# Cross attention of a Perceiver block: 2048 scores at a time in one group of four PSUM banks, and another order of its first slots

## What is computed

```python
# x 256x512 (normalised), cond 4096x512, 16 heads of 32
q = (x @ Wq + bq) * 32**-0.5;  k, v = split(cond @ Wkv + bkv)
q = quantise(q, per row);  k = quantise(k, per row)     # round(x / s) * s, s = absmax / 127
v = quantise(v, per column over the tokens)
a = softmax(q @ k.T)                                     # per head 256 x 4096
a = round(a / (max(a) / 255)) * (max(a) / 255)
out = (a @ v) @ Wp + bp
```

## Time and profile before

| what | us |
|---|---|
| median of 3 runs (lowest, highest) | 582.43 (581.07, 583.52) |
| span of the profiled execution | 582.8 |
| busy in it: PE, DVE, ACT, POOL | 531.9, 457.6, 364.7, 28.4 |
| first scores of the cross attention to its last exponentials' start | 128.95 to 361.46 |

### The profile page before, as it was taken

The page is one execution under the profiler, slowest core; times in us unless marked ns, Lnnn a source line. Parts: engine busy times, 40 slices in busy tenths (PEclk is TensorE's granted clock), DMA queues, the critical chain, the costliest instruction groups (busy, mean ns, idle before and its releaser), DMA issues. The chain is left out here.

```text
span 582.8 us, 10649 instructions
## 1 busy us (share of the span) xinstructions
PE 531.9 (91%) x4283; PEld 333.8 (57%) x4286; DVE 457.6 (79%) x858; ACT 364.7 (63%) x431; POOL 28.4 (5%) x28
## 2 busy tenths in 40 slices
PE   3999999999899999999998788699999899996995
PEld 2444555543566656665665565488884565652582
DVE  2599999966899989998999797401593889878995
ACT  5624656464799889988998788400343753586342
POOL 0300000000300200030005100000000000000000
PEclk9999999999999999999998788899999999997999
DMA  8723300042345435553556459603938204300000
GB/s 319 264 74 87 130 1 1 0 142 85 119 148 182 165 107 176 166 168 112 160 177 241 170 165 432 265 1 95 319 163 341 106 0 180 111 0 0 2 2 36
DMA packets 20145, 78.84 MB, mean 135 GB/s; under 512 B 2176, under 2 KB 3200, under 8 KB 16896
## 3 DMA queue, kind: packets, MB, share of 16 engines
q1 hardware_dynamic: 20096, 78.16, 37.8%
HBM read 75.27 MB, written 0.79 MB: 131 GB/s over the span
## 5 line engine op out<-in xcount | busy, mean ns | idle before, releaser
L1122 DVE CUSTOM_DVE_ANT_0 arena<-ps,arena 128x1024 f32<-128x1024 f32 x128 | 152.5, 1220 | 16.2 <-issue 7.7
L1530 ACT ACTIVATE arena<-arena,small 128x4096 int16<-128x4096 f32 x32 | 121.5, 3798 | 2.5 <-DVE small L1135 2.4
L600 PE MATMUL ps<-arena 128*128 128x512 f16 x384 | 100.1, 380 | 0.0
L641 PE MATMUL ps<-small,arena 128*128 128x128 bf16 x1024 | 81.7, 225 | 8.1 <-DVE arena L1142 4.8
L566 PE MATMUL ps<-arena 128*128 128x512 f16 x384 | 85.2, 379 | 1.2 <-DVE arena L1053 1.2
L641 PEld LDWEIGHTS ps<-small,arena 128*128 128x128 bf16 x1024 | 61.1, 100 | 17.8 <-issue 6.9
L1537 ACT ACTIVATE arena<-ps 128x512 int32<-128x512 int32 x96 | 56.9, 593 | 21.7 <-PE ps L641 21.3
L815 PE MATMUL ps<-arena 128*128 128x256 f32 (+1 forms) x288 | 67.3, 397 | 0.7 <-ACT arena L1619 0.7
L815 PEld LDWEIGHTS ps<-arena 128*128 128x128 f32 x288 | 55.7, 194 | 11.8 <-issue 3.3
L566 PEld LDWEIGHTS ps<-arena 128*128 128x128 f16 x384 | 37.2, 98 | 43.6 <-issue 1.5
L657 PEld LDWEIGHTS ps<-arena 128*128 128x128 f16 x1024 | 43.0, 97 | 30.1 <-issue 8.2
(11 more groups left out here) (172 smaller groups left out, 729.5 us busy)
## 6 DMA issues: line engine op xcount, KB each, us to landing
arena<-key_scales SPq DMA_DIRECT2D x64, 512.0 KB, 5.0
arena<-in_ctxT SPq DMA_DIRECT2D x8, 1024.0 KB, 6.8
arena<-in_wg SPq DMA_DIRECT2D x4, 1024.0 KB, 7.2
arena<-in_wo SPq DMA_DIRECT2D x2, 2048.0 KB, 11.6
arena<-in_wu SPq DMA_DIRECT2D x4, 1024.0 KB, 6.9
arena<-in_wd SPq DMA_DIRECT2D x4, 1024.0 KB, 5.8
arena<-in_wuq SPq DMA_DIRECT2D x1, 3072.0 KB, 24.9
arena<-in_wkr SPq DMA_DIRECT2D x1, 2048.0 KB, 13.9
```

The costliest lines, as they stand in the source:

```text
L600: last = pe.matmul(ps[:, bank, :], wv16[wpart][:, k, g * P:(g + 1) * P], ctx16[cpart][:, k, tok], start=(k == 0 and i == 0), stop=(k == KC ...
L641: last = pe.transpose(ps[:, bank, :].bitcast(BF16)[:, b * P:(b + 1) * P], p16[u % 2][:, (8 * q + b) * P:(8 * q + b + 1) * P].bitcast(BF16) ...
L1122: dve.tensor_tensor_reduce(sc[:, u % 2, i * SCW:(i + 1) * SCW], ps[:, 2 * (n % 2):2 * (n % 2) + 2, :].rearrange("p a b -> p (a b)"), skb[: ...
L1530: act.activation(p16[u % 2], sc[:, u % 2, :], ACT.Exp, bias=ebias[:, u % 2:u % 2 + 1], scale=sq[:, i:i + 1], accum_out=rsum[:, u:u + 1]).t ...
```

## The change

A unit's scores are made in two calls of 2048 keys: four matmuls on the four groups of 32 array rows into banks 0 to 3. There is only this one group of four banks, so call n waits for scaling n-1. DVE scales 2048 at once; the second operation starts its maximum from the result of the first, so `score_max` goes. The ring is 3 loads of 1024 KB. A call of the second half writes the whole region of the int16 exponentials, so it waits for all four transposes of unit u-2. The first three slots are written out by hand (`first_slots`): group 1's first part is projected there, parts 1 to 5 in slots 3 to 7, and parts 6 and 7 both in slot 8. DVE instead of ACT reads three projections of group 0 out, and for groups 1 to 3 stores three of the four v quarters (before two). `turn_values(g, 0)` comes earlier in its slot, `turn_p` and `values` are otherwise in their places.

```diff
-RING = 5
+SPAN = 2 * SCW
+HALVES = 2
+RING = 3
...
-        ORDER = (2, 3, 0, 1)
+        ORDER = (1, 0)
...
+            if s <= 1:
+                return [(0, j, FREE_BANKS[j]) for j in (2 * s, 2 * s + 1)]
+            if s <= SLOTS:
+                return [(1, j, 7) for j in ((6, 7) if s == SLOTS else (s - 2,))]
...
-                if n >= 2:
-                    pe.wait_ge(scu, n - 1)
+                    pe.wait_ge(scu, n)
-                for a in range(2):
-                    row = slice(HD * (2 * cp + a), HD * (2 * cp + a + 1))
-                    last = pe.matmul(ps[:, 2 * (n % 2) + a, :], qT4[row, h, t * P:(t + 1) * P],
+                for a in range(4):
+                    row = slice(HD * a, HD * (a + 1))
+                    last = pe.matmul(ps[:, a, :], qT4[row, h, t * P:(t + 1) * P],
...
                 dve.tensor_tensor_reduce(
-                    sc[:, u % 2, i * SCW:(i + 1) * SCW],
-                    ps[:, 2 * (n % 2):2 * (n % 2) + 2, :].rearrange("p a b -> p (a b)"),
-                    skb[:, load % RING, :], 1.0, -3.0e38, ALU.mult, ALU.max,
+                    sc[:, u % 2, i * SPAN:(i + 1) * SPAN],
+                    ps[:, 0:4, :].rearrange("p a b -> p (a b)"),
+                    skb[:, load % RING, :], 1.0, smax[:, u % 2, 0:1] if k else -3.0e38, ALU.mult, ALU.max,
                     smax[:, u % 2, k:k + 1]).then_inc(scu, 1)
-
-            def score_max(u):
-                dve.wait_ge(scu, (u + 1) * NCH)
-                dve.tensor_reduce(mfin[:, u % 2:u % 2 + 1], smax[:, u % 2, :], AX, ALU.max).then_inc(mf, 1)
...
+                if len(steps) == 2:
+                    store_projected_values(*steps[0])
+                if half == 0:
+                    store_values(group, 0)
```

More of the change, by code:

```diff
@@ L398, in turns @@
[L398 to L403, removed]
+            p = [("p", s - 2, 2), ("p", s - 2, 3), ("p", s - 1, 0), ("p", s - 1, 1)]
+            if s == 2:
+                out = p[:2] + [("v", 0, c) for c in range(NCH)] + p[2:]
+            elif half == 0:
+                out = p[:2] + [("v", g, 0), p[2], ("v", g, 1), p[3]]
+            elif half == 1:
+                out = [p[0], ("v", g, 2), p[1], ("v", g, 3)] + p[2:]
+            else:
+                out = p
@@ L730, in _, with project_part @@
+            first_slots()
+            for s in range(3, UNITS + 2):
                 now = s < UNITS
[L731 to L733 removed]
+                late = s - 2 < UNITS
+                prev = s - 1 < UNITS
+                pieces = [(g, j, bank, k) for g, j, bank in value_steps(s) for k in range(KC)]
+                each = len(pieces) // 4
                 group, half = values_turned_in(s)
[L735 removed]
+                def project_part(n):
+                    for g, j, bank, k in pieces[n * each:(n + 1) * each]:
+                        project_values(g, j, bank, [k])
@@ L736, in _ @@
                 if now:
                     scores(s, 0)
-                    scores(s, 1)
-                for g, j, bank in steps[:1] if s == 0 else []:
-                    project_values(g, j, bank, range(KC))
-                if late:
-                    turn_p(s - 2, 2)
-                for g, j, bank in inline:
-                    project_values(g, j, bank, [0])
-                if late:
-                    values(s - 2, 0)
+                turn_p(s - 2, 2)
+                project_part(0)
@@ L756, in _ @@
                     project_first((s - FIRST_OUT - 3) // 2, [2])
-                for g, j, bank in steps[1:2] if s == 0 else []:
-                    project_values(g, j, bank, range(KC))
-                for g, j, bank in inline:
-                    project_values(g, j, bank, [1])
-                if late:
-                    values(s - 2, 1)
-                if half == 1:
-                    turn_values(group, 3)
-                if now:
-                    scores(s, 3)
+                values(s - 2, 1)
+                if half is not None:
+                    turn_values(group, 3 if half else 0)
                 if s in (FIRST_OUT, FIRST_OUT + 1):
@@ L1218, in _ @@
                     add_first(0)
-                if now:
-                    scale_scores(s, 1)
-                if s == 1:
-                    for g, j, _ in last[2:]:
-                        max_values(g, j)
-                    scale_values(group)
                 if late:
```

260 lines of the change are left out of this document (152 added, 108 removed).

## The result

The changed kernel takes 588.41 us (median of 4 runs, 587.43 to 588.85) beside 582.97 for the kernel before (4 runs, 581.07 to 584.10): ratio 1.0095, 95% interval 1.0071 to 1.0119. It is slower by 5.4 us. The forecast was 588.9 us, with a chance of 0.69 for slower. The 66 runs of the kernel before that were made beside the experiments lie between 580.85 and 586.67 us, so two single runs can differ by 1%, not only by the 0.3% named at the start.

What follows compares the result with a forecast made beforehand. PE, DVE and ACT are nearly full, with a PE-ACT loop setting plain slots. Terms -1.2 + 3.1 - 2.2 + 3.3 + 0.5 + 3.0 = +6.5 gave 589.3 us span, 588.9 median; range 585 to 593, wider 580.5 to 597.

Steps and rivals of the forecast that it cites:

- Plain slots: Sixteen plain steps with a projection: beat 6.46 to 6.38 us, held by a PE-ACT loop of waits; -1.2 us.
- The first rival: Plain slots: the PE-ACT loop does not bind, beat is PE's 6.13 us; 577.9 us in all, chance 0.13.
- The scaling: DVE's scaling of 2048 keys at once: 2.2 us, between 2.0 and 2.44.
- Slot 8: Group 1's parts 6 and 7 both here: twelve more matmuls and a wait for the shared bank; +3.1 us.
- First slots: Opening slots shed 2.6 us of matmuls and 1.3 of scores but gain waits; -2.2 us, bounds 0 and -3.9.
- unit 3 near 164: Sign that the forecast is right: unit 3's exponentials start near 164 us in the profile.
- Boundaries: First two slots of each value group: PE waits for the late value scale, then for DVE's copy and store; +3.3 us.
- The clock: PE's stops of 2.5 and 1.9 us bring one clock fall each in groups 1 and 2; +3.0 us, bounds 0 and 9.
- The third rival: Clock falls often, also in the opening slots and last six units: four more falls, +6, 595 us; chance 0.17.
- The tail and the stage ahead: Slots from unit 26 on, apart from load delays, and the stretch before the first projection of v: no change.
- Loads: Ring loads of 1024 KB land 5.8 us after issue, late only after head 12; +0.5 us, bounds 0 and 1.3.
- the fourth rival: Ring of three starves: 1024 KB broadcasts land in 7.5 us, delaying scalings; +7 on the forecast, 596 us; chance 0.05.

Runs made afterwards that it cites:

- The wide scores alone: Kernel before with only the 2048-key scores in four banks, single scaling and ring of three added; projections and turned values unmoved: 582.39 us, ratio 0.9996.
- the placement alone: Changed kernel with the earlier kernel's 1024-key scores and ring of five, keeping the moved projections, first slots and turned values: 591.78 us, ratio 1.0147.
- the fourth run: Changed kernel with last maximum and value scale made ahead of the first scores' scaling on DVE in a value group's first slot: 586.54 us, ratio 1.0055.
- the third run: Changed kernel with each value projection's last quarter ahead of the first turned probabilities on PE, its ACT read-out ahead of their first copy: 589.54 us, ratio 1.0105.
- two edits: Changed kernel with earlier last projection quarter and read-out, plus value scale ahead of the first scaling in a group's first slot: together 583.44 us, ratio 1.0013.

## Why the prediction was right, point by point

**Plain slots: right, and shown.** 6.46 became 6.40, not PE's 6.13. The forecast took the loop for 6.38; its four links measured 6.40. (Its 16 x 0.08 is 1.3, not 1.2; 1.0 came.) That it is the loop is shown by the pair of runs with it cut: 6.22 with wide scores, 6.46 without. The first rival (the loop doesn't bind) is out.

**The scaling.** The forecast took 2.2 us from bounds of 2.0 and 2.44; the page says 2.29 and 2.35:

```profile
L1165 DVE CUSTOM_DVE_ANT_0 arena<-ps,arena,small 128x2048 f32<-128x2048 f32 x32 | 75.2, 2349 | 5.8 <-PE ps L651 5.0 <-DMA arena<-key_scales 0.8
L1165 DVE CUSTOM_DVE_ANT_0 arena<-ps,arena 128x2048 f32<-128x2048 f32 x32 | 73.3, 2292 | 7.1 <-PE ps L651 3.4 <-DMA arena<-key_scales 1.4 <-issue 1.0
```

The Trainium skill, "VectorE: DVE Perf Modes", section "The TRN2 errata", gives (N+151)/0.96 ns for an addition of two fp32 tensors of N columns, 2291 at 2048. The multiply-and-maximum here agrees when it starts from a constant (2292).

**Slot 8: right.** +3.25 came for +3.1: twelve matmuls of 2.6, and 0.90 until ACT has emptied the bank (194.61 in PE's rows), for which 0.8 was taken.

**First slots: mis-sized.** -2.2 was taken, -0.9 came. The wide scores alone gave -0.4 there (48.53 us), the placement alone -1.1 (47.75). The size is loose: five of the profiled kernels have the same code up to unit 2 (the changed one and four of the experiments on it), and from the first projection to unit 2 they take 40.44 to 42.86 us, 41.5 on average, where the kernel before took 42.44. The step that failed is the choice within 0 to -3.9: the new waits in series were named but not priced. PE's rows show three of 1.67 to 1.78 us, two for the one scaling in front of each scores call and one for DVE's store; in the first of them the scaling itself had stood 0.91 us for its key scales. The sign "unit 3 near 164" came true (163.89) by luck: 1.3 of its 2.2 us lie ahead of the first slots.

**Boundaries: right in place, mechanism and size.** Groups 2 and 3 gave +0.9 and +0.7 (forecast +0.8 each); group 1, which holds the fall of the clock, +3.5 (forecast 1.65 and 1.5). PE's stop was 2.39 where 2.5 was forecast, 1.79 where 1.9 was. In the second boundary slot PE waits for the two DVE operations that the forecast named, in group 1 1.18 us for the copy and 1.29 for the store. That the scale is late because it is queued behind the long scaling is shown by the fourth run.

**The clock: half right.** One fall in group 1 as forecast, none in group 2. In the third run the same stop of 1.79 us in group 2 was followed by half clock. How often a run falls is not something the profiles settle, since each shows one execution; by the estimate from the mean clocks of all runs half clock takes 15.1 us in the changed kernel and some 13.4 before, so about 1.7 more, not 3.0. The third rival's many falls (595) did not come.

**The tail and the stage ahead** were taken as nothing and gave -1.1 and -1.3. Before, some 17 us at half clock lie between 315 and 360 us; after, some 14 lie there and 3.4 at 204, so in these two executions the total is equal: the profile of the kernel before is of one of its slower executions. The 1.3 us of the stage ahead are the spread between executions: the first projection starts anywhere from 115.72 to 117.25 us in the eleven profiles, 115.82 and 117.16 in two kernels with the same code up to there (the one before, and it with the loop cut).

**Loads: no loss where it was forecast.** Behind head 12 the scaling waits 0.47 us for key scales (at 324 us), 0.88 before (at 319 us), and in a plain slot never. But 0.91 and 0.77 stand ahead of the first two scalings, where the forecast had none. 1024 KB land sooner than 512 KB did, so the fourth rival had no ground:

```profile
arena<-key_scales SPq DMA_DIRECT2D x32, 1024.0 KB, 4.8
```

So the total was right with errors that cancel, which is luck. On the span 6.5 was forecast and 4.1 came: the first slots were 1.3 too good, boundaries and clock together 1.2 too dear, and tail, loads and stage ahead came out 2.9 better. Against that, the span was carried to the median with 0.4 taken off, where 1.5 had to be added (586.9 to 588.4).

## What to carry to other kernels

When three engines are nearly full, follow one unit through the loop of who waits for whom before counting what one engine saves: here 0.33 us of PE's work per slot was worth 0.05 until the loop was cut, and 0.24 after. An operation twice as long is paid for by what is queued behind it on its engine; look where a rarely run step (here the value scale) starts work on an otherwise idle engine. A gain in plain slots and a stop at a boundary are not independent: two edits that gained nothing and 1.9 us alone gained 5.0 together. And where single stops of 1 to 2 us decide over the clock, compare the mean granted clock of all runs before one profile is taken for the kernel.

## What the runs showed of the hardware that was not expected

- The scaling that starts its maximum from a tensor of one column per partition takes 57 ns longer than the one that starts it from a constant (2349 and 2292, 32 of each). That the start value is the reason is not shown by itself; before, where all four scalings of a unit start from a constant, the 128 of them lie between 1212 and 1226.
- A broadcast of 1024 KB lands 4.8 us after issue (median), one of 512 KB 5.0.
- A stop of PE of one length goes with either clock. In the changed kernel one of 1.79 us was followed by 1.00 in group 2 and by 0.52 in group 3. The third and fourth run were made on one chip and have the same code up to unit 2; there a stop of 1.67 us, for the same store, was followed by 1.00 in the third and 0.50 in the fourth. Third, then fourth run:

```profile
155.96 0.55 PE L678 MATMUL ps<-arena 128*128 128x32 f16 x16 [1.67 <-DVE arena L1145]
...
157.00:160.00 3.00, 2.45 (x47) 1.83 (x45) 1.01 (x3) 2.00 (x3) 0.00 (x0) 1.00 0.02 5
```

```profile
153.27 0.55 PE L678 MATMUL ps<-arena 128*128 128x32 f16 x16 [1.67 <-DVE arena L1145]
...
155.00:158.00 3.00, 2.84 (x37) 2.24 (x38) 0.33 (x3) 1.90 (x4) 0.00 (x0) 0.50 0.02 5
```

So the length of a stop alone does not decide it, and the forecast's step from two stops to two falls had no firm ground.
